# Attention with q and k split in two halves: the head innermost in the written products, one plain copy for each half, three reads of the stacks, and the first scores behind the value product

## What is computed

```python
q = _ln((x @ Wq + bq).reshape(b, s1, H, HD), qn_w, qn_b)
kv = jnp.concatenate([y_main @ Wk + bk, y_main @ Wv + bv], axis=-1).reshape(b, s2, H, 2 * HD)
k, v = _ln(kv[..., :HD], kn_w, kn_b), kv[..., HD:]
ctx = _attn(qT, k.transpose(0, 2, 1, 3), v.transpose(0, 2, 1, 3))
ctx_dca = _attn(qT, k_dca..., v_dca...)      # the last 16 context rows, with weights of their own
return (ctx + ctx_dca) @ Wo + bo
...
x = x + _L0_xattn_ref(_layernorm(x, axis=-1), ctx_1024, ...)
x = x + _L0_ffn_ref(_layernorm(x, axis=-1), L0_ffn_kernel, L0_ffn_bias)
```

## Time and profile before

| | us |
|---|---|
| median of 3 runs | 570.86 (570.58 to 571.43) |
| the profiled execution | 571.64 |
| its span, first to last instruction | 569.8 |
| TensorE busy | 375.6 (66%), mean granted clock 0.812 |
| VectorE busy | 291.5 (51%) |
| ScalarE busy | 210.6 (37%) |
| GpSimd busy | 191.3 (34%) |
| moved by DMA | 55.92 MB, mean 98 GB/s |

### The profile page before, as it was taken

How to read it: one execution, slowest core, us unless ns; L and a number is a source line. 1 busy time by engine, 2 the same in 40 slices (tenths; PEclk the granted TensorE clock), 3 DMA queues, 4 the chain that set the end, 5 groups by cost and what they waited for, 6 DMA issues and landing times.

```text
span 569.8 us, 7677 instructions
## 1 busy us (share of the span) xinstructions
PE 375.6 (66%) x2383; PEld 298.7 (52%) x2383; DVE 291.5 (51%) x813; ACT 210.6 (37%) x389; POOL 191.3 (34%) x285
## 2 busy tenths in 40 slices
PE   0257718479494959495959594959494949486751
PEld 0025515378383747374747473748383838375630
DVE  1663512775363646364747463736463646353542
ACT  1044412245252525252625252625352525242212
POOL 9000400234151424243434243434343333332332
PEclk9997566789796979697979597959797989775775
DMA  8510050231414151515151515151515050404001
GB/s 277 210 55 30 26 171 0 96 101 50 147 54 144 46 171 46 169 40 177 41 175 46 171 38 177 39 177 33 183 35 181 27 161 27 160 25 143 20 1 55
DMA packets 39524, 55.92 MB, mean 98 GB/s; under 512 B 7736, under 2 KB 26428, under 8 KB 39484
## 3 DMA queue, kind: packets, MB, share of 16 engines
q1 hardware_dynamic: 37952, 54.02, 29.2%
q10 hardware_dynamic: 1532, 1.42, 0.8%
HBM read 33.93 MB, written 21.50 MB: 97 GB/s over the span
## 4 chain that ended last, share of the span: by engine, by line
DMA 33%; PE 24%; issue 12%; SPq 4%; ACT 2%; POOL 2%; DVE 1%; ACTq 0%; POOLq 0%; DVEq 0%
DMA k_stack<-stack_scratch 18%; DMA stack_scratch<-k_lo 15%; PE bank L1066 14%; PE bank L1139 4%; SPq L311 3%; PE bank L1277 2%; PE bank L1189 1%; ACT k_hi L526 1%; PE bank L1204 1%; PE bank L1181 1%; PE bank L1170 1%; POOL wq_raw L461 0%; ACT wkv_raw L622 0%; DMA out<-finals 0%; POOL f_small L426 0%
## 5 line engine op out<-in xcount | busy, mean ns | idle before, releaser
L890 DVE TENSOR_REDUCE neg_max<-bank 128x4 f32<-128x448 f32 (+1 forms) x128 | 45.2, 414 | 112.6 <-PE bank L1139 112.6
L439 POOL TENSOR_TENSOR k_lo<-wkv_raw,k_hi 128x448 f16<-128x448 f32 x16 | 17.0, 1061 | 252.6 <-issue 237.9
L1139 PE MATMUL bank<-k_stack,q_stack 128*128 128x128 f16 x256 | 26.9, 268 | 107.7 <-issue 95.2
L1139 PEld LDWEIGHTS bank<-k_stack,q_stack 128*128 128x128 f16 x256 | 22.0, 122 | 116.9 <-issue 116.4
L1170 PE MATMUL bank<-v_aug,prob_store 128*128 128x66 f32 x512 | 72.3, 288 | 16.1 <-ACT prob_store L611 12.6
L1170 PEld LDWEIGHTS bank<-v_aug,prob_store 128*128 128x128 f32 x512 | 67.9, 204 | 20.1 <-ACT prob_store L611 14.4
L611 ACT ACTIVATE prob_store<-bank,exp_scale 128x512 f32<-128x512 f32 x64 | 42.0, 681 | 32.4 <-PE bank L1151 32.4
L526 ACT ACTIVATE cT_hi<-bank 128x512 fp32r<-128x512 f32 x16 | 9.6, 597 | 116.6 <-PE bank L1277 116.6
L454 POOL TENSOR_TENSOR finals<-seg_out 128x128 f32<-128x128 f32 x64 | 31.1, 486 | 39.4 <-DVE seg_out L903 36.1
L622 ACT ACTIVATE wkv_raw<-bank,affine 128x448 f32<-128x448 f32 (+1 forms) x32 | 22.4, 748 | 45.2 <-PE bank L1204 45.1
L1015 DVE TENSOR_REDUCE f_small<-wo_raw 128x1 f32<-128x512 f32 x16 | 11.0, 686 | 54.1 <-POOL wo_raw L430 54.1
(11 more groups left out here) (195 smaller groups left out, 963.0 us busy)
## 6 DMA issues: line engine op xcount, KB each, us to landing
k_stack<-stack_scratch SPq DMA_DIRECT2D x16, 512.0 KB, 7.2
q_stack<-stack_scratch SPq DMA_DIRECT2D x16, 512.0 KB, 3.8
x_in<-in_x SPq DMA_DIRECT2D x16, 256.0 KB, 4.1
stack_scratch<-k_hi SPq DMA_DIRECT2D x32, 128.0 KB
stack_scratch<-k_lo SPq DMA_DIRECT2D x32, 128.0 KB
stack_scratch<-q_hi SPq DMA_DIRECT2D x32, 128.0 KB
stack_scratch<-q_lo SPq DMA_DIRECT2D x32, 128.0 KB
out<-finals SPq DMA_DIRECT2D x16, 256.0 KB, 4.2
```

What stands on the lines that cost most here:

```text
L890: v.tensor_reduce(neg_max[:, HG * gr:HG * (gr + 1), seg], s4[:, :, lo:hi], AX.X, ALU.max, negate=True).then_inc(max_ready.sem, 1)
L1139: last = mm(bank[4 + gr % 2][:, P * h:P * (h + 1)], q_stack[:, b.parity, h, gr], k_stack[:, b.parity, h, gr], start=True, stop=True)
```

## The change

- `k_t`, `q_t` and the same product of the 16 extra rows are written with the head innermost (d * 4 + g in place of g * 32 + d). The gains and shifts (`norm_rows`) are laid out to match.
- After the transposes a row of `k_hi` and its like is d * 4 + g, which is just the order of rows that the stack wants. Each half is copied to DRAM once, 128 x 512 onto 128 x 512: four copies of 128 KB a batch, not eight.
- The doubling moves to the reads. k is read as 64 rows of 4 KB, taken twice (a leading count of 2 with a stride of 0); q_stack is read in two parts, each 32 rows taken twice, and each waits for its own half alone.
- The scores of groups 0 and 1 and their maxima move from the end of step t into step t+1: on TensorE ahead of the transposes of y and x, on VectorE behind the split of cT and ahead of the Newton steps.

```diff
-            def put(N, which, slots, t, done):
-                for slot in slots:
-                    sp.dma_start(stack_scratch[N.parity, which, HD * slot:HD * (slot + 1)].rearrange("d g n -> g d n"),
-                                 flat(t)).then_inc(done.sem, 16)
+            def twice(parts):
+                return parts.unsqueeze(0).to_broadcast([2, parts.shape[0], HG * D])
+            def rows(t):
+                return t.rearrange("p g c n -> p (g c n)")
...
+                    put = stack_scratch[N.parity]
+                    pair = put.rearrange("w s (d g) n -> w (s d) (g n)", g=HG)
...
-                    put(N, 0, (0, 2), k_hi[:], k_put)
+                    sp.dma_start(put[0, 0], flat(k_hi[:])).then_inc(k_put.sem, 16)
...
-                    put(N, 1, (2, 3), q_lo[:], q_put)
+                    sp.dma_start(put[1, 1], flat(q_lo[:])).then_inc(qlo_put.sem, 16)
...
                     sp.wait_ge(*k_put.of(N))
-                    sp.dma_start(k_stack[:, N.parity].rearrange("p g c n -> p g (c n)"), stack_scratch[N.parity, 0]
-                                 ).then_inc(kstack_in.sem(N), 16)
-                    sp.wait_ge(*q_put.of(N))
-                    sp.dma_start(q_stack[:, N.parity].rearrange("p g c n -> p g (c n)"), stack_scratch[N.parity, 1]
-                                 ).then_inc(qstack_in.sem(N), 16)
+                    sp.dma_start(rows(k_stack[:, N.parity]), twice(pair[0])).then_inc(kstack_in.sem(N), 16)
+                    for part in range(2):
+                        sp.wait_ge(*(qhi_put, qlo_put)[part].of(N))
+                        sp.dma_start(rows(q_stack[2 * HD * part:2 * HD * (part + 1), N.parity]),
+                                     twice(pair[1, HD * part:HD * (part + 1)])).then_inc(qstack_in.sem(N), 16)
...
-                    v.tensor_tensor(grouped(k_t[0:MAIN]), grouped(k_raw[0:MAIN, N.parity]),
+                    v.tensor_tensor(head_inner(k_t[0:MAIN]), by_head(k_raw[0:MAIN, N.parity]),
                                     wide(qk_small[0:MAIN, 5, 1]), ALU.mult).then_inc(kt_ready.sem, 1)
...
                 if Bt is not None:
                     if Bt.first():
                         pe.wait_ge(sel_made.sem, 4)
+                    pe.wait_ge(*kstack_in.of(Bt))
+                    pe.wait_ge(*qstack_in.of(Bt))
+                    scores(0)
+                    scores(1)
...
-                if N is not None:
-                    pe.wait_ge(*kstack_in.of(N))
-                    pe.wait_ge(*qstack_in.of(N))
-                    scores(0)
-                    scores(1)
```

More of the change, by code:

```diff
@@ L119, in xattn_ffn @@
         ones3 = sb("ones3", [P, P], BF16)
-        norm_rows = sb("norm_rows", [1, 6, HG, HD])
+        norm_rows = sb("norm_rows", [1, 6, HD, HG])
         affine = sb("affine", [P, 6])
@@ L465, in step @@
                     low(k_lo, k_n, k_hi, kn_ready, khi_ready, k_put, klo_ready, MAIN)
-                    low(q_lo, q_n, q_hi, qn_ready, qhi_ready, q_put, qlo_ready, P)
+                    low(q_lo, q_n, q_hi, qn_ready, qhi_ready, qlo_put, qlo_ready, P)
                     if N.first():
@@ L730, in grouped, with by_head, head_inner @@
                 return ap.rearrange("p (h d) -> p h d", d=HD)
+            def by_head(ap):
+                return ap.rearrange("p (c g d) -> p c g d", g=HG, d=HD)
+            def head_inner(ap):
+                return ap.rearrange("p (c d g) -> p c g d", g=HG, d=HD)
             def wide(ap):
-                return ap.unsqueeze(2).to_broadcast([ap.shape[0], ap.shape[1], HD])
+                return ap.rearrange("p (c g) -> p c g", g=HG).unsqueeze(3).to_broadcast([ap.shape[0], XC, HG, HD])
             def centre(heads, chunks, means, done):
@@ L883, in maxima @@
                 def maxima(gr):
[L884 to L887, removed]
+                    dve.wait_ge(*scores_ready.of(Bt, gr + 1))
+                    if Bt.has(1):
+                        dve.wait_ge(*maxlo_ready.of(Bt.back(1)))
                     s4 = bank[4 + gr % 2][:, :].rearrange("p (h n) -> p h n", n=P)
@@ L933, in step @@
                     low_part(cT_lo, cT_hi, bank[6][:, :], chi_ready, attn_ready, C, clo_ready)
+                if Bt is not None:
+                    maxima(0)
+                    maxima(1)
                 if N is not None:
@@ L1097, in setup_columns @@
                 for n in range(6):
-                    last = mm(bank[6][:, n:n + 1], norm_rows[0:1, n].rearrange("a g d -> a (g d)"), ident[0:1, 0:1],
+                    last = mm(bank[6][:, n:n + 1], norm_rows[0:1, n].rearrange("a d g -> a (d g)"), ident[0:1, 0:1],
                               start=True, stop=True)
@@ L1131, in scores @@
                 def scores(gr):
-                    b = N if gr < 2 else Bt
                     if gr >= 2:
-                        pe.wait_ge(*max_ready.of(b, 2 * (gr - 1)))
-                    elif b.has(1):
-                        pe.wait_ge(*probs_ready.of(b.back(1), gr + 3))
+                        pe.wait_ge(*max_ready.of(Bt, 2 * (gr - 1)))
+                    elif Bt.has(1):
+                        pe.wait_ge(*probs_ready.of(Bt.back(1), gr + 3))
                     for h in range(HG):
-                        last = mm(bank[4 + gr % 2][:, P * h:P * (h + 1)], q_stack[:, b.parity, h, gr],
-                                  k_stack[:, b.parity, h, gr], start=True, stop=True)
+                        last = mm(bank[4 + gr % 2][:, P * h:P * (h + 1)], q_stack[:, Bt.parity, h, gr],
+                                  k_stack[:, Bt.parity, h, gr], start=True, stop=True)
                     last.then_inc(scores_ready.sem, 1)
@@ L1305 @@
     scratch = nc.dram_tensor("dca_scratch", (256, shape[2]), FP32, kind="Internal").ap()
-    stacks = nc.dram_tensor("stack_scratch", (2, 2, 128, 4, 512), FP16, kind="Internal").ap()
+    stacks = nc.dram_tensor("stack_scratch", (2, 2, 2, 128, 512), FP16, kind="Internal").ap()
     xattn_ffn(nc, *args, out, scratch, stacks)
```

19 lines of the change are left out of this document (8 added, 11 removed).

## The result

The changed kernel takes 699.51 us (699.34 to 700.01, 4 runs) against 570.72 us: 1.2257 times as long, 95% interval 1.2236 to 1.2278. The forecast was 660 (632 to 732). The profiled execution has a span of 697.7 us.

What follows compares the result with a forecast made beforehand. The round trip of q and k through DRAM sets the 28.9 us period; copies give back about 8 us, order about 2, reads take some 17, making 35.0 a batch. With start and tail: 660 us (632 to 732).

Steps and rivals of the forecast that it cites:

- T to kT: From the start of a batch's first scores on TensorE to its kT transposes: 5.8 us, against 7.65 before.
- landing, and SyncE's step: The k_lo copy reaching DRAM, 1.7 us, then SyncE's step to the k read, 0.07 us.
- fixed part, data, TensorE's start: Stack reads: 2.2 us before data, 21.3 us for 512 KB on each of two engines, 0.07 us until first scores.
- Rival C: Copies to DRAM get no faster, held by something other than their pattern: 730 us; chance 2 in 100.
- signs of being wrong: DMA share 0.5 or more during reads, TensorE idle under 3 us a batch, or an engine outside 20 to 26 GB/s.
- The strided write of k_t: On VectorE, the strided write may cost up to 0.7 us more for each of two, hidden by the output projection.
- TensorE's idle time: TensorE stands idle for 12 us or so a batch, behind the cT transposes and value product.
- Loads behind the reads: Other loads on SyncE wait behind the stack reads on the two busy engines; costed at nothing.
- Start and tail: First scores start at 91.2 us in the first batch, 123.8 in batch 1; the tail stays at 45.2 us.
- Rival A: Stack reads use all sixteen engines: period 21.5 us, end near 450 us (440 to 480); chance 7 in 100.
- The break-even: 15.2 us left for 1 MB of reads, 69 GB/s or 2.8 engines; from three on, no longer slower.
- The order: Moving first scores and maxima into the next step on TensorE and VectorE gives back about 2 us a batch.

Runs made afterwards that it cites:

- e10: The changed kernel with x, y and residual loads and the result store cut to fewer columns, output no longer the reference's: 687.14 us, ratio 1.206 to the kernel before.
- e1: The changed kernel with each doubled read split into plain reads of one copy each (k as two, q as four): 450.44 us, ratio 0.795 to the kernel before.
- e8: The changed kernel with eight copies out and k and q each read in one transfer of 4 x 32 rows: 561.86 us, ratio 0.983 to the kernel before.
- e3: The kernel before with only the first scores and maxima moved into the next step: 536.48 us against 566.64.
- e4: The changed kernel with the first scores and maxima put back to the end of the step, doubled reads kept: 727.24 us, ratio 1.282 to the kernel before.
- e2: e1 with the first scores and maxima put back to the end of the step: 445.70 us, ratio 0.780 to the kernel before.
- e9: e2 with GpSimd's addition of bias to the residual moved behind the rounding of the feed-forward input: 437.19 us, ratio 0.768 to the kernel before.

## Why the prediction was right, and where its terms were off

The mechanism, the sign and the two engines were right, and 699.5 lies in the range. The forecast of 660 is 40 us low. By the prediction's own steps, in the period from 393.72 to 431.61 and in the mean of 14 periods (batch 1 at 129.70 to batch 15 at 654.41):

| step | forecast | this period | mean |
|---|---|---|---|
| T to kT | 5.8 | 6.51 | 6.64 |
| kT to the copy of k_hi | 2.59 | 2.58 | 2.59 |
| to the copy of k_lo | 1.27 | 1.48 | 1.23 |
| landing, and SyncE's step | 1.77 | 1.78 | 2.11 |
| fixed part, data, TensorE's start | 2.2 + 21.3 + 0.07 | 25.54 | 24.92 |
| sum | 35.0 | 37.89 | 37.48 |

- **Copies.** 1.7 us, as taken from the result store. Rival C is out: 1 KB writes to DRAM are not slow when all engines carry them.
- **The reads.** The term that was most off: 24.92 us in the mean against 23.57, 1.35 us too little 16 times, 22 of the 40 us. It is made of errors that partly cancel. Start and end, drawn from one 32 KB read on quiet queues, are 2.9 us and not 2.27; the slowing of q beside other transfers, 2.0 us, had been put at nothing; the data took 19.9 us at 26.4 GB/s and not 21.3 at 24.6. That the two largest of them, 1.4 and 2.0 us, have opposite signs is luck for the forecast. A rate above 26 was also one of the prediction's signs of being wrong; the windows (26 to 26.5 GB/s) and the line (26.6) lie just above it, and what they contradict is the rate, not the two engines. By the figure of the Trainium skill (page "DMA: Bandwidth & Descriptors", section "Specifications", about 27 GiB/s an engine) the estimate was 610, and it fell further off: the windows show 26 to 26.5 GB/s while the data flows.
- **SyncE's step to the k read.** 0.34 us more than forecast in the mean, some 5 us in all: the read leaves 1.75 to 3.10 us after the k_lo copy.
- **T to kT.** 0.7 us short in this period, 0.84 in the mean, some 12 us of the 40 over 14 periods. Ahead of the first scores TensorE has stood for over 11 us, and the low clock then lasts longer than in the kernel before. There the mean of 0.61 over 3.98 us is 3.1 us at the lower level; here the two windows behind T give 3.28 us of it and, with 0.80 over 3.00 us, another 1.2:

```profile
393.72:397.00 3.28, 3.28 (x23) 3.21 (x24) 2.56 (x8) 0.98 (x2) 0.00 (x0) 0.50 0.06 21
397.00:400.00 3.00, 3.00 (x12) 2.35 (x12) 2.96 (x8) 0.00 (x0) 0.00 (x0) 0.80 0.02 5
```

  The 1.4 us more at half the speed cost the 0.7. The output projection starts slow too: 0.77 us for its first product where the earlier trace rows has 0.48.
- **The strided write of k_t.** Within its bound, and hidden. VectorE's row:

```profile
396.35 1.08 DVE L955 TENSOR_TENSOR wq_raw<-k_raw,qk_small 112x512 f32<-112x512 f32 x1
```

  1.08 us against 0.69: +0.39 of the 0.7 allowed. It ends at T + 3.7, and the kT transposes come at T + 6.5 and wait for nothing.
- **TensorE's idle time.** 12.36 us where "12 us or so" was written.
- **Loads behind the reads.** Costed at nothing, which was wrong for the reads themselves. x_in takes 15.9 us to land, and SyncE stands 4 to 5 us over some issues (406.62 and 410.71 above), but no other engine waits for them; the price is in the q reads, 2.0 us a batch while these transfers run, of which e10 shows 0.65 to be theirs.
- **Start and tail.** First T at 93.47 (91.2): the same stretch of the read, 25.8 us for 23.57. Batch 1 at 129.70 (123.8). The tail is 697.7 - 654.41 = 43.3 us (45.2).
- **Rival A** was no result of this change, but its price was right: e1 gives 450.44 us and 21.3 us a period where 450 and 21.5 were worked out.
- **The break-even** of three engines was too low. With the measured means the steps without data are 17.8 us (6.64, 2.59, 1.23, 2.11 and 5.2), which leaves 11.1 of the 28.9 for 1 MB: 94 GB/s, or about 3.5 engines at 26.6. That is an estimate; e8 with four, and with eight copies, is 1.7% faster than the kernel before.
- **The order.** Its gain, put at about 2 us a batch, is 2.0 in e3 and 1.3 in e4. That the same order costs about 2% once the reads are fast (e1 against e2) was not foreseen: the prediction looked for what TensorE's scores wait for, and not for the waits of TensorE that the first scores had filled.

## What to carry to other kernels

Look at the outermost count of both patterns of a DMA before its bytes: a count of 2 in front of 64 rows, repeated or real, puts 256 KB on each of two engines, and one plain transfer for each copy moves the same bytes 249 us sooner here. Price such a read by bytes on the busiest engine, with what is queued ahead of it there, plus its start. And what a change of order is worth depends on the wait that binds: the same move gained 4 to 5% beside slow transfers and lost 2% beside fast ones.

## What the runs showed of the hardware that was not expected

- A read on two engines has no long start of its own: 2.9 us of start and end against about 2.6 on sixteen. Its q part ran at 0.187 us a packet beside other transfers, its k part at 0.155 to 0.158.
- k_t, written with innermost elements 16 bytes apart, costs 1.08 us for 112 x 512 f32, against 0.69 us for the plain one. Its sources are read through one more dimension too, and no run separates the two.
- In the changed kernel, TensorE's granted clock is at 0.50 for some 4.5 us of work after 12 us of standing still, against 3.1 us in the kernel before.
- The granted clock is a gain that is easily missed: 0.756 over the span of the changed kernel and 0.93 in e9, where TensorE hardly stands still.
- A VectorE instruction with three sources took 1.86 us instead of 0.74 whenever GpSimd's addition of 128 x 512 ran beside it (e9).
